# Two pipelined attentions: the output projection from three bf16 products of split halves in place of one float32 product, with the work of every engine set out in a new order

## The reference

```python
x = x + jnp.tanh(g_xattn[0]) * _L0_xattn_ref(_layernorm(x), ctx_1024, Wq, Wkv, Wo, bo)
x = x + jnp.tanh(g_ffn[0])   * _L0_ffn_ref(_layernorm(x), w_router, w1, w2, w3)
x = x + jnp.tanh(g_xattn[1]) * _L1_xattn_ref(_layernorm(x), ctx_1024, ctx_1024, ..., Wg, bg, Wo)
x = x + jnp.tanh(g_ffn[1])   * _L1_ffn_ref(_layernorm(x), w1, conv_w, conv_b, w2)
# both attentions: 16 heads of width 16, softmax(q k / 4) v, then
out = out.transpose(0, 2, 1, 3).reshape(B, Nq, C)
return out @ Wo + bo          # the second: return y * sigmoid(qn @ Wg.T + bg) @ Wo.T
```

## Time and profile before

| | |
|---|---|
| Time, median of 3 runs | 2454.98 us (2453.3 to 2462.52) |
| The profiled execution | 2457.4 us, span of its instructions 2455.6 us |
| PE busy | 1749.3 us (71%) |
| DVE busy | 1685.6 us (69%) |
| ACT busy | 1404.8 us (57%) |
| POOL busy | 1232.2 us (50%) |
| First attention | 0 to about 487 us |
| Second attention | about 1230 to 1762 us |

### The profile page before, as it was taken

How to read it: one execution, slowest core, us unless ns; L and a number is a source line. 1 busy time by engine, 2 the same in 40 slices (tenths; PEclk the granted TensorE clock), 3 DMA queues, 4 the chain that set the end, 5 groups by cost and what they waited for, 6 DMA issues and landing times. The chain is left out here.

```text
span 2455.6 us, 49999 instructions
## 1 busy us (share of the span) xinstructions
PE 1749.3 (71%) x14877; PEld 1401.0 (57%) x14877; DVE 1685.6 (69%) x3884; ACT 1404.8 (57%) x2826; POOL 1232.2 (50%) x1351
## 2 busy tenths in 40 slices
PE   5999999853316999999739999999534444444444
PEld 3777777543315999999627888888422222222222
DVE  4888888564431333323238999999589988888887
ACT  4888888621102444444337777777366666666664
POOL 2444444246663222222267777776055555555553
PEclk8999999955557999999969999999866666666666
DMA  3122222264332223223254555554200000000000
GB/s 102 60 79 91 80 92 80 64 206 162 123 125 84 85 86 90 86 85 90 63 106 108 117 118 111 111 114 97 87 9 26 26 26 26 26 26 26 26 26 17
DMA packets 182023, 194.05 MB, mean 79 GB/s; under 512 B 24400, under 2 KB 171600, under 8 KB 180880
## 3 DMA queue, kind: packets, MB, share of 16 engines
q1 hardware_dynamic: 157328, 157.88, 20.9%
q0 software_dynamic: 24576, 34.62, 7.0%
HBM read 118.20 MB, written 74.24 MB: 78 GB/s over the span
## 5 line engine op out<-in xcount | busy, mean ns | idle before, releaser
L1728 POOL TENSOR_TENSOR e_h_lo<-e_h 128x256 bf16<-128x256 f32 (+1 forms) x213 | 130.2, 611 | 326.9 <-DVE e_h L1937 326.9
L1937 DVE TENSOR_TENSOR e_h<-e_s,e_ps_ab 128x256 f32<-128x256 f32 (+1 forms) x213 | 89.4, 420 | 294.2 <-ACT e_s L1763 294.2
L1956 PE MATMUL e_ps_ab<-e_xt_hi,e_w_hi 128*128 128x256 bf16 (+1 forms) x852 | 233.2, 274 | 0.2 <-issue 0.2
L1956 PE MATMUL e_ps_ab<-e_xt_hi,e_w_lo 128*128 128x256 bf16 (+1 forms) x852 | 233.0, 273 | 0.0
L1956 PE MATMUL e_ps_ab<-e_xt_lo,e_w_hi 128*128 128x256 bf16 (+1 forms) x852 | 232.9, 273 | 0.0
L2185 POOL TENSOR_TENSOR f_y<-f_tap 128x512 f32<-128x512 f32 x128 | 163.2, 1275 | 108.5 <-ACT f_tap L2208 108.5
L2403 PE MATMUL f_ps_y<-f_w_q,f_zq 128*128 128x256 bf16 x512 | 114.9, 418 | 119.4 <-DVE f_zq L2333 119.4
L2188 POOL TENSOR_TENSOR f_y<-f_y,f_tap 128x512 f32<-128x512 f32 x128 | 188.8, 1475 | 14.8 <-POOL f_y L2185 9.2
L1695 POOL DMA_INDIRECT sent_rows<-e_xn,e_slot x128 | 140.2, 1095 | 87.0 <-DVE e_seen L1870 48.8
L1763 ACT ACTIVATE e_s<-e_ps_ab 128x256 f32<-128x256 f32 (+1 forms) x213 | 81.3, 382 | 152.1 <-PE e_ps_ab L1956 152.1
L2403 PEld LDWEIGHTS f_ps_y<-f_w_q,f_zq 128*128 128x128 bf16 x512 | 71.5, 145 | 156.9 <-DVE f_zq L2333 128.7
(11 more groups left out here) (422 smaller groups left out, 6247.8 us busy)
## 6 DMA issues: line engine op xcount, KB each, us to landing
e_xe<-sent_rows SPq DMA_DIRECT2D x71, 272.0 KB, 2.8
back_rows<-e_yo SPq DMA_DIRECT2D x71, 256.0 KB, 2.1
x_rows<-a_x SPq DMA_DIRECT2D x64, 256.0 KB, 2.2
a_xt<-in_xT SPq DMA_DIRECT2D x32, 256.0 KB, 2.9
a_xa<-in_x SPq DMA_DIRECT2D x32, 256.0 KB, 3.8
a_xr<-in_x SPq DMA_DIRECT2D x32, 256.0 KB, 2.8
e_xa<-x_rows SPq DMA_DIRECT2D x8, 1024.0 KB, 10.7
a_xa<-x_rows SPq DMA_DIRECT2D x32, 256.0 KB, 3.3
```

Of the source, the lines that this page charges most:

```text
L1728: nc.gpsimd.tensor_tensor(h_lo[0:k, b.par, c, :], h[0:k, b.par, c, :], h_hi[0:k, b.par, c, :], ALU.subtract).then_inc(mg.sem, 1)
L1937: nc.vector.tensor_tensor(h[0:k, b.par, c, :], s[0:k, c, :], ps_ab[0:k, c, N:2 * N], ALU.mult).then_inc(mh.sem, 1)
L1956: last = nc.tensor.matmul(to, left, right, start=(i == 0), stop=(i == len(terms) - 1))
```

## The change

The result and `wo` are split in bf16 halves as q and kv were already. `oh` is the high half (ACT), `ol` the low half (DVE), `woh` and `wol` are made once by DVE ahead of the steps. PE makes `proj` of a batch from 12 bf16 products of 128x256 in place of 4 in float32. In the first attention `oh` is taken straight from PSUM and `ot` goes; in the second `ot` stays, and `oh` and `ol` are made from it.

The lists of all engines are new in both attentions. In the first, `q_hi`, `q_lo`, the transposes and `rope_k` go from step n to step n + 1 of a batch, the first two scores `ms0`, `ms1` stand at the end of PE's list, and SP issues `ca` ahead of `xa`. In the second, a batch's statistics, its normalised input, `q`, the scores and the projection come one step later than before or more (`proj` and `fin` under `at(6)`), `cl` goes from POOL to DVE, `v` from ACT to DVE, `k2a` and `k2b` from DVE to ACT. The banks of PSUM are shared out anew.

```diff
+        woh, wol = [sb(n, [P, KC, D], BF16) for n in ("woh", "wol")]
+        oh, ol = [sb(n, [P, KC, N], BF16) for n in ("oh", "ol")]
...
             def step(at):
-                b = at(4)
-                if b is not None:
-                    nc.sync.dma_start(xr[:, b.par, :, :], x_t[b.n]).then_inc(r_ld[b.par], 16)
                 b = at(0)
                 if b is not None:
                     gp0.wait(sp, at(2), "xl")
                     nc.sync.dma_start(xt[:, b.par, :, :], a["xT"][b.n]).then_inc(t_ld[b.par], 16)
+                    nc.sync.dma_start(ca[:, b.par, :, :], a["ctxT"][b.n]).then_inc(c_ld[b.par], 16)
                     dve0.wait(sp, at(2), "bn")
                     nc.sync.dma_start(xa[:, b.par, :, :], x_t[b.n]).then_inc(x_ld[b.par], 16)
-                    gp0.wait(sp, at(2), "cl")
-                    nc.sync.dma_start(ca[:, b.par, :, :], a["ctxT"][b.n]).then_inc(c_ld[b.par], 16)
...
+            nc.vector.tensor_copy(woh[:, :, :], wo[:, :, :]).then_inc(s_fold, 1)
+            dve.wait_ge(s_fold, 8)
+            nc.vector.tensor_tensor(wol[:, :, :], wo[:, :, :], woh[:, :, :], ALU.subtract).then_inc(s_fold, 1)
...
+                    pe4.wait(act, b, "oT")
+                    nc.scalar.activation(oh[:, :, :].rearrange("p k n -> p (k n)"), ps_c[:, :], ACT.Copy).then_inc(act4.sem, 1)
...
+                    act4.wait(dve, b, "oh")
+                    nc.vector.tensor_tensor(ol[:, :, :].rearrange("p k n -> p (k n)"), ps_c[:, :], oh[:, :, :].rearrange("p k n -> p (k n)"), ALU.subtract).then_inc(dve4.sem, 1)
...
+                    dve4.wait(pe, b, "ol")
...
-                        last = product(ps_b[:, t * D:(t + 1) * D], terms(ot, slice(t * P, (t + 1) * P), wo))
+                        last = product(ps_d[:, t * D:(t + 1) * D], halves(oh, ol, slice(t * P, (t + 1) * P), woh, wol))
...
-                        last = product(ps_a[:, t * D:(t + 1) * D], terms(ot, slice(t * P, (t + 1) * P), wo))
+                        last = product(ps_b[:, t * D:(t + 1) * D], halves(oh, ol, slice(t * P, (t + 1) * P), woh, wol))
```

More of the change, by code:

```diff
@@ L564, in step @@
             def step(at):
+                b = at(4)
+                if b is not None:
+                    freed(pe, (dve4, at(5), "ol"), (act1, at(2), "k2b"), (dve4, at(5), "of0"))
+                    for g in range(H // GH):
+                        last = nc.tensor.transpose(ps_c[:, g * P:(g + 1) * P], raw[:, g, 0 * P:1 * P], ident[:, :])
+                    last.then_inc(pe4.sem, 1)
                 b = at(2)
                 if b is not None:
-                    dve1.wait(pe, b, "top6")
+                    dve2.wait(pe, b, "top0")
                     for j in range(2):
@@ new lines, in step @@
+                b = at(3)
+                if b is not None:
+                    act3.wait(pe, b, "ex6")
+                    for g in (0, 1):
+                        for j in range(GH):
+                            last = nc.tensor.matmul(ps_e[j * VW:(j + 1) * VW, 0, (g % 2) * N:(g % 2 + 1) * N],
+                                                    v1[0:S, b.par, GH * g + j, :], probs[0:S, GH * g + j, :], start=True, stop=True)
+                    last.then_inc(pe3.sem, 1)
+                b = at(2)
@@ L847, in attention_second @@
-        dve3 = Signal(sem(tag + "dve3"), "m_hi m_lo spread")
-        dve4 = Signal(sem(tag + "dve4"), "rec1 rec0 of0 of1 ot")
-        dve5 = Signal(sem(tag + "dve5"), "fin")
-        act1 = Signal(sem(tag + "act1"), "xt xh ct ch q_hi")
-        act2 = Signal(sem(tag + "act2"), "k_hi v q2a tanh")
-        act3 = Signal(sem(tag + "act3"), "mt ex0 ex1 ex2 ex3 ex6 ex5 ex4")
-        act4 = Signal(sem(tag + "act4"), "ex7 raw1 raw0")
-        pe1 = Signal(sem(tag + "pe1"), "xT cT q")
-        pe2 = Signal(sem(tag + "pe2"), "kv qTb qTa kT ms3 ms0 ms2 ms1 ms4 g ms5 ms6 ms7")
@@ new lines, in attention_second @@
+        dve2 = Signal(sem(tag + "dve2"), "cl")
+        dve3 = Signal(sem(tag + "dve3"), "k_lo q_lo v q2b")
+        dve4 = Signal(sem(tag + "dve4"), "top3 top2 top1 top4 top5 top0 top7 top6 m_hi m_lo spread")
+        dve6 = Signal(sem(tag + "dve6"), "rec1 rec0 of0 of1 ot ol fin")
+        act2 = Signal(sem(tag + "act2"), "xt ct ch xh")
+        act3 = Signal(sem(tag + "act3"), "k_hi q_hi k2a k2b q2a")
+        act4 = Signal(sem(tag + "act4"), "mt")
+        act5 = Signal(sem(tag + "act5"), "tanh ex0 ex3 ex4 ex1 ex2 ex5 raw0 ex7 ex6 raw1")
@@ L1244, in step @@
+                if b is not None:
+                    act5.wait(pe, b, "ex6")
                     for g in (2, 3):
@@ L1335, in step @@
[L1335 to L1344 removed]
+                    dve4.wait(pe, b, "spread")
```

1394 lines of the change are left out of this document (701 added, 693 removed).

## The result

The changed kernel takes 2489.23 us (median, 2486.55 to 2492.64), the kernel before 2455.44 us beside it; the ratio is 1.0133, interval 1.0108 to 1.0158. It is slower by about 34 us, 33 by the ratio. Forecast were 2434 us and a gain.

What follows compares the result with a forecast made beforehand. PE was taken to bound the second attention, a ring through `fin` and the context's load the first. Gains of 15 and 6 us off the profiled 2457.4 gave 2436, or 2434 us for the median; range 2413 to 2450.

Steps and rivals of the forecast that it cites:

- The product: Both attentions: twelve bf16 products take 1.31 us, so PE loses 0.48 and 0.42 us a batch.
- First attention, steady: First attention's 26 even steps: each 13.1 us, 0.5 less than before, giving 13.8 us in all.
- the new ring: First attention, changed: `fin` through SP and context load to `ch` 5.2 us, back to `fin` 7.9, step 13.1.
- the old ring: First attention before: `ch` to end of `fin` 7.73 us, on to the next `ch` 5.90, the whole 13.63 step.
- Second attention, steady: Second attention's 27 even steps: PE, without idle time, stays the limit and goes from 14.83 to 14.4 us.
- rival D: Second attention: store waits for `fin` ahead of the next load; two-step chain 27.0 us, whole 2470 us; chance 0.10.
- The rule against it: Second attention: DVE's two-input `ol` and `cl` may block POOL through shared ports, at worst 1.9 us over two steps.
- the slack: Second attention: the load chain is hidden under PE's steps by 1.8 us over two steps.
- decision point: Second attention: the load chain must reach 15.6 us a step to make the whole kernel slower.
- The edges: Second attention's ends: first `fin` at 1325, 6.4 us later, and the last four `fin` intervals 39 us in all.

Runs made afterwards that it cites:

- loads_first_1: The changed kernel with the first attention's result store one step later, behind the next loads, and the residual's load behind that store: 2463.79 us, ratio 1.0025.
- xr_later: The changed kernel with only the first attention's residual load moved from ahead of the next loads to behind them: 2467.35 us, ratio 1.0007.
- loads_first_2: The changed kernel with the second attention's result store one step later, behind the loads of x, places and context: 2463.30 us, ratio 1.0026.
- ol_later: old_prod_loads with the first attention's `ol` moved behind `m_lo` in DVE's list, where POOL is idle: 2444.41 us, ratio 0.9944.
- mix_again: The same kernel as mix, run once more on a third chip: 2432.75 us, ratio 0.9861.
- mix: First attention as changed with its loads ahead of the store, second in its order of before with the bf16 products: 2434.62 us, ratio 0.9860.
- both_loads: The changed kernel with results stored one step later, behind the loads, in both attentions: 2444.45 us, ratio 0.9905.
- old_prod_loads: The kernel before, orders kept, with the bf16 products in both attentions and the first attention's loads ahead of the store: 2466.94 us, ratio 1.0003.
- fin_early: The changed kernel with the first attention's `fin` earlier in DVE's list, SP's order as changed: 2475.43 us, ratio 1.0040.

## Why the prediction was wrong

**The product** was right, 1.31 us as forecast:

```profile
301.47 0.27 PE L550 MATMUL a_ps_d<-a_woh,a_oh 128*128 128x256 bf16 x1
...
302.78 0.43 PE L619 MATMUL a_ps_e<-a_q,a_k 128*120 128x256 bf16 x2
```

In the second attention PE, where it is the limit, has 14.49 us a step for a forecast of 14.4.

**First attention, steady: the failed step is the length of the new ring.** I named the ring rightly (cutting it in loads_first_1 and xr_later moved the step at once) and made it 5.2 + 7.9 = 13.1 us. It measured 5.45 + 8.4 = 13.85 in the mean of 22 rounds (5.8 + 8.4 in the one shown). The larger part is the way from `ch` to `fin`: I went by ACT's list up to `pv0`; the way is DVE's, which has what it waits for 1.6 us after `ch`, and then thirteen groups of its list without a gap, 6.0 us, before `fin`. The smaller part is a reading of the old ring. I had put the next `ch` of the kernel before at 314.90, from the mean step; it stands at 315.34:

```profile
315.34 0.40 ACT L323 ACTIVATE a_ch<-a_ca 128x240 bf16<-128x240 f32 x1 [1.19 <-DMA a_ca<-in_ctxT]
```

So from `fin` to `ch` were 6.3 us and not 5.9 in that round, 6.25 in the mean of 22, beside 7.4 from `ch` to `fin`. The change took 0.8 off the first (one issue less, 0.5, and the context's load landing 0.3 sooner), a little more than the 0.7 that I gave it, and put 1.0 on the second: 13.65 became 13.85, and the steady part lost 0.2 us a step in place of gaining 0.5.

**Second attention, steady: the failed step is that PE stays the limit.** The mechanism that I priced as rival D at 27.0 us over two steps took 31.0. Term by term: issue 1.1 for 0.7; load to first gather 4.7 for 3.6, because the gathers also wait for the places, which the change issues 0.6 us behind the 256 KB load of x: their 2 KB land 3.7 us after the issue. Before, they were issued 0.6 to 0.9 us behind a 256 KB store and ahead of the loads, and took 2.0 (the DMA tables of change and of before):

```profile
a_where<-places SPq DMA_DIRECT2D x32, 2.0 KB, 3.7
```
```profile
a_where<-places SPq DMA_DIRECT2D x32, 2.0 KB, 2.0
```

From there to the last gather 9.8 for 8.65, 0.5 of it ahead of the first gather and 0.4 a wait of GpSimd on VectorE (see "The rule against it"); the last landing 5.5 for 4.4 (I took the median of all gathers, and needed the time until DVE begins behind the last one); from the statistics on 9.9 for 9.6. None is large; the slack was 1.8 us and they sum to 4.0. I gave D a chance of 0.10 and a decision point of 15.6 us a step; it came to 15.45, and with no gain from the first attention that was enough: 27 steps of 15.4 in place of 14.4 are 27 us. loads_first_2 cut this chain, and PE set the step again.

**The edges** were near: first `fin` at 1324.9 for 1325, though 2.8 of the 6.3 us of delay are handed down by the first attention, and the last four intervals 43.8 us for 39. That is some 5 us too little at the end and 3 too much at the start.

**The rule against it.** I read POOL's `cl` at 1249 ns in the median, against 642 at the least, as VectorE holding POOL back. For that row the runs speak for another cause: what stands directly behind a pair of gathers shows 0.55 to 0.62 us more, whatever it is (POOL before, then changed; `xl` moved behind the pair, the first addition too):

```profile
L968 POOL TENSOR_TENSOR a_xl<-a_xt,a_xh 128x512 bf16<-128x512 f32 x19 | 21.9, 1151 | 40.4 <-ACT a_xh L1026 40.4
L946 POOL TENSOR_TENSOR a_ve<-a_mv,a_oneeps 128x3 f32<-128x3 f32 x19 | 4.0, 212 | 0.7
```
```profile
L955 POOL TENSOR_TENSOR a_xl<-a_xt,a_xh 128x512 bf16<-128x512 f32 x19 | 33.6, 1768 | 0.0
L969 POOL TENSOR_TENSOR a_ve<-a_mv,a_oneeps 128x3 f32<-128x3 f32 x18 | 13.8, 765 | 0.0
```

Its record starts while the gather's still runs, so it is partly a matter of how the two overlap in the trace. The conflict itself exists, and in both directions. DVE's `ol` takes 1.72 us beside `xb`, which began first, and 0.68 away from it. The Trainium skill ("SBUF — State Buffer", Who interferes with whom) says that VectorE and GpSimd share a port pair under an exclusive lock; by that rule it is GpSimd that holds the lock there, and the row and ol_later agree with it. In the second attention of the change VectorE begins first, and a GpSimd instruction of 0.19 us takes until VectorE's is through:

```profile
1506.31 0.68 DVE L1206 TENSOR_TENSOR a_ol<-a_ot,a_oh 128x512 bf16<-128x512 f32 x1
...
1506.42 0.62 POOL L977 TENSOR_TENSOR a_pace_n<-a_half 128x1 f32<-128x1 f32 x1
...
1520.85 0.19 POOL L977 TENSOR_TENSOR a_pace_n<-a_half 128x1 f32<-128x1 f32 x1
```

From 1400 to 1685 us this happens to `pace_n` in 8 of 18 steps (0.54 to 0.68 us); each time it ends 0.05 to 0.08 us behind `ol` or behind DVE's bf16 copy ahead of it (L1202). So the rule was at work in rival D's chain as I feared, but small: 0.4 of its 4.0 us, where I had allowed up to 1.9.

**Where the forecast gain went.** PE's relief is real (loads_first_1, loads_first_2: 12.76 and 14.49 us). It was turned into a wait: on SP, for `fin`, in front of the loads of both attentions. With the product's relief, the first attention's new list and without that wait the kernel takes 2433 to 2444 us on chips where before took 2466 (mix_again, mix, both_loads). With the old list the loads alone give nothing (old_prod_loads); there `ol` has to leave `xb`'s side as well (ol_later).

**Left open.** What holds fin_early at 13.2 us and ol_later at 13.09. And the second attention of both_loads was not separated into chip and ring: 14.49 on one chip (without the first's edit), 14.86 on another, where the unchanged one had 14.98.

## What to carry to other kernels

A queue that issues both stores and loads must not wait for a result ahead of the next loads, when no load needs it: store one step later, behind them. It was worth 0.5 to 1.0 us a step in three of the four loops where it was tried, for a few moved lines (both attentions of the change, the first of the kernel before); in old_prod_loads another limit stood in front and it gave nothing. When a ring's slack is small (1.8 us of 28.8 here), take each term from the instance on the ring (the last gather, the small transfer behind the big one, every instruction in front of it in its engine's list), not from a median, from the mean step or from another engine's list. And ask for every instruction added to a list what it waits for and who is queued behind it, before its own duration.

## What the hardware showed that I had not expected

- A 2 KB load issued 0.6 us behind a 256 KB load landed 3.7 us after its issue (3.2 in loads_first_2), and 2.0 after it where a 256 KB store had been issued 0.6 to 0.9 us ahead of it and no load. A 120 KB load landed in 3.5, 3.1 and 2.5 us with three, two and one load of 256 KB between it and the store.
- A two-input VectorE instruction on SBUF took 1.72 us beside a GpSimd addition of the same size that had begun 0.1 us sooner, and 0.68 away from it. The other way round, a GpSimd instruction of 0.19 us took 0.62 where VectorE's had begun 0.1 us sooner.
- The second attention of before, unchanged and with PE busy 285 of 285 us at a granted clock of 1.00, took 14.84 us a step in one profile and 14.98 in another, on another chip, while the first attention's PE-bound step was 12.76 on three chips. Why was not looked into.
